# A later place for GpSimd's product of step and u and its mark, and ScalarE's normalization behind its tile's side work

## The reference, cut to what matters

```python
xf = silu(conv(x @ in_proj_w.T, conv_w))            # 512 channels
delta, B, C = split(xf @ x_proj_w.T)                # rank 16, 16 states each
dt = softplus(delta @ dt_proj_w.T + b)
y = selective_scan(u=xf, dt, A, B, C, D) * silu(res)
x = layernorm(x + (y + y_backward) @ out_proj_w.T)  # first norm
...
logits = layernorm(x)*g+b  @  slot embeddings       # 1024 slots
x = layernorm(x + combine(experts(dispatch(x))))    # second norm
```

## Time and profile before

| what | value |
|---|---|
| median of 3 runs | 5855.48 us (5845.51 to 5856.24) |
| the profiled execution's own time | 5838.37 us |
| its span, first to last instruction | 5836.5 us |
| mean granted TensorE clock | 0.929 |
| busy: TensorE, VectorE, GpSimd, ScalarE | 86%, 79%, 75%, 70% of the span |
| GpSimd, dtu (L624) | 65 times, 2179 ns |
| GpSimd, g (L643) and v (L652) | 1026 and 768 times, 2369 and 2368 ns |

### The profile page before, as it was taken

One profiled execution on the slowest core, in us unless ns is written; L12 is line 12 of the kernel. 1 busy time (PEld: TensorE's weight loads), 2 busy tenths in 40 slices (PEclk: granted clock), 3 DMA queues, 4 the chain that ended last, 5 costly groups with the idle time before them and its releaser, 6 DMA issues. The chain is left out here.

```text
span 5836.5 us, 50669 instructions
## 1 busy us (share of the span) xinstructions
PE 5031.1 (86%) x14640; PEld 2563.0 (44%) x14640; DVE 4622.5 (79%) x4109; ACT 4081.5 (70%) x6431; POOL 4362.3 (75%) x2136
## 2 busy tenths in 40 slices
PE   6888888888888888888888878787889787999999
PEld 3444443434343434344444434343434344656578
DVE  6898989898989898989898989898989992222235
ACT  4888888888888888888888888887878883111100
POOL 4898989898989999999999999999998981000000
PEclk8999989898989999999898989898989898999999
DMA  2444434444444444444444444344444442343356
GB/s 88 128 133 127 136 124 134 128 133 128 133 129 129 132 133 131 129 128 133 126 131 128 135 127 134 127 132 131 124 138 124 137 126 78 99 138 122 98 171 216
DMA packets 555604, 755.29 MB, mean 129 GB/s; under 512 B 124091, under 2 KB 272443, under 8 KB 553277
## 3 DMA queue, kind: packets, MB, share of 16 engines
q1 hardware_dynamic: 540765, 737.36, 41.1%
q10 hardware_dynamic: 14560, 14.68, 0.8%
HBM read 662.04 MB, written 89.82 MB: 129 GB/s over the span
## 5 line engine op out<-in xcount | busy, mean ns | idle before, releaser
L643 POOL TENSOR_TENSOR g_ring<-dtu,b_ring 128x1024 f32<-128x1024 f32 x1026 | 2418.9, 2369 | 271.6 <-DVE e_ps L1000 246.1
L1000 DVE TENSOR_TENSOR_SCAN e_ps<-e_ps,g_ring 128x1024 f32<-128x1024 f32 x1024 | 2343.3, 2288 | 11.8 <-POOL g_ring L643 11.8
L1156 PE MATMUL y_ps<-v_ring,ident 128*128 128x512 f32 x3088 | 1626.3, 636 | 235.1 <-DVE res_gate L983 189.9
L652 POOL TENSOR_TENSOR v_ring<-z_ring,c_ring 128x1024 f32<-128x1024 f32 x768 | 1816.7, 2368 | 0.0
L796 ACT ACTIVATE e_ps<-dt,a_neg 128x512 f32<-128x512 f32 x2050 | 1327.9, 680 | 458.1 <-DVE v_own L1022 298.3
L806 ACT ACTIVATE f_ring<-rsum,consts,a_neg_half 128x512 f32<-128x512 f32 x2052 | 1550.9, 805 | 36.7 <-DVE e_ps L1013 33.7
L1156 PEld LDWEIGHTS y_ps<-v_ring,ident 128*128 128x128 f32 x3088 | 589.3, 204 | 889.6 <-issue 807.4
L1013 DVE SCALAR_TENSOR_TENSOR z_ring<-f_ring,e_ps 128x1024 f32<-128x1024 f32 x768 | 935.6, 1218 | 50.8 <-issue 1.7
L1156 PE MATMUL y_ps<-v_own,ident 128*128 128x512 f32 x1028 | 533.8, 614 | 0.0
L1089 PE MATMUL side<-u,conv_diag 128*128 128x512 f32 x1088 | 494.6, 597 | 20.7 <-ACT disp_ring L757 11.3
L1326 ACT ACTIVATE x_act<-x_ps,x_bg 128x512 f32<-128x512 f32 x128 | 87.9, 687 | 570.2 <-PE x_ps L1385 570.2
(11 more groups left out here) (133 smaller groups left out, 5180.1 us busy)
## 6 DMA issues: line engine op xcount, KB each, us to landing
b_ring<-bc_scr SPq DMA_DIRECT2D x1027, 256.0 KB, 3.7
c_ring<-bc_scr SPq DMA_DIRECT2D x1025, 256.0 KB, 3.4
pT_scr<-rowT_ring SPq DMA_DIRECT2D x136, 256.0 KB, 4.1
m_pT<-pT_scr SPq DMA_DIRECT2D x16, 2048.0 KB, 8.5
sT_scr<-sT_ring SPq DMA_DIRECT2D x272, 64.0 KB, 2.8
x_xT<-sT_scr SPq DMA_DIRECT2D x16, 1024.0 KB, 9.3
eo_scr<-x_eo SPq DMA_DIRECT2D x32, 512.0 KB, 5.1
m_eo<-eo_scr ACTq DMA_DIRECT2D x14, 1024.0 KB, 7.1
```

The lines of the kernel that those rows point to most:

```text
L643: pool.tensor_tensor(g_ring[:, k], dtu[d][:], both(b_ring[:, k:k + 1]), ALU.mult).then_inc(g_done, 1)
L652: pool.tensor_tensor(v_slot(i), z_ring[:, k], both(c_ring[:, k:k + 1]), ALU.mult).then_inc(v_pool, 1)
L1000: dve.tensor_tensor_scan(e, e, g, 0.0, ALU.mult, ALU.add).then_inc(scan_done, 1)
L1156: pe.matmul(y_ps[:, t % 2], ident[:], v, start=(t % (TILES // PAIRS) < 2), stop=True, skip_group_check=True).then_inc(v_used, 1)
```

## The change

The product dtu is issued four tiles behind its slot and the mark six tiles behind it (three and five before). At tile 29 ScalarE goes through the side work first and normalizes behind it.

```diff
-    DTU_LAG, RSUM_LAG, CUT_LAG = 3, 3, 5
+    DTU_LAG, RSUM_LAG, CUT_LAG = 4, 3, 6
...
                     if t == ROUGH_TILE:
                         rough_rstds(b)
+                    for s in range(SLOTS):
+                        side_step(at, s, t - tile_of[s])
                     if t == APPLY_TILE:
                         normalize(b)
-                    for s in range(SLOTS):
-                        side_step(at, s, t - tile_of[s])
```

## The result

The changed kernel takes 5798.62 us (median of 4 runs, 5796.90 to 5799.63) against 5852.56 for the kernel before (5845.51 to 5856.24): a ratio of 0.9909, 95% interval 0.9892 to 0.9926. That is 54 us less where 29.7 were forecast, and 2.4 us under the low end of the range. The profiled executions stand 40.0 us apart.

What follows compares the result with a forecast made beforehand. A loop across GpSimd, ScalarE, VectorE and TensorE, 297.0 us a round, was taken as the bound; 1.5 + 0.48 = 1.98 us, times 15, is 29.7, so 5855.5 - 29.7 = 5825.8 us, range 5801 to 5849.

Steps and rivals of the forecast that it cites:

- no wait ahead of dtu: GpSimd's 4.86 us wait for the softplus ahead of dtu of dt0_1 would be nearly gone.
- 3.34 back ahead of g(53): About 3.3 of GpSimd's 4.86 us would come back as a wait for VectorE ahead of g(53).
- normalize without a wait: ScalarE's wait for GpSimd's last norm instruction ahead of normalize would be gone or below 0.2 us.
- 1.13 ahead of scan(16): VectorE's wait for the tanh would go, and one of about 1.2 us for ScalarE would appear ahead of scan(16).
- 0.55 more at the row maximum: VectorE's wait at the row maximum, which hangs on TensorE's rows, would grow by half a microsecond.
- the two other products: On GpSimd, the later dtu of dt0_3 and of dt1_1 were each taken at nothing.
- The sum of the chain: Everything behind ScalarE's normalize comes 1.5 (GpSimd's lead) + 0.48 (the tanh) = 1.98 us earlier in each of fifteen sequences.
- The second rival, a lost lead: GpSimd's lead never reaches normalize; only the tanh's slot is left, 0.48 x 15 = 7 us, 5848; chance 0.19.
- TensorE's clock: TensorE's two speed levels, looked at in in0 (5.40 or 3.70 us), were taken to give no change.
- the first rival: TensorE gets faster on top: in0 at its quick level in every sequence, 25 us more, 5801; chance 0.13.
- against the median the sum is 5855.5 - 29.7: The profiled execution lay 17.1 us below its kernel's median; the forecast against the median was 5825.8.
- sequence 0, for which I counted nothing: A dt0_1 of the loop lies ahead of normalize only in sequences 1 to 15, so sequence 0 got no gain.

Runs made afterwards that it cites:

- the order alone: Kernel before with only normalize moved behind the side work, the lags left at 3 and 5: 5827.89 us, ratio 0.9965.
- before_again: The kernel before, run unchanged for a second profile: 5846.76 us, ratio 1.0001.
- the fed kernels: Kernel before and changed kernel, each with zero-weight products ahead of six pieces of TensorE's side work: first pair 5744.19 and 5726.09 us.
- before_fed: Kernel before plus zero-weight products ahead of six pieces of TensorE's side work: 5744.19 us, ratio 0.9809.
- after_late11: Changed kernel plus one more VectorE maximum over 1024 columns in each sequence, result unused: 5823.76 us, ratio 0.9949.
- before_fed2: Kernel before plus zero-weight products, more than in before_fed ahead of xnT_0 (6 for 5) and rows_0 (7 for 4): 5742.45 us, ratio 0.9822.

## Why the prediction was wrong

**What held.** Every step about the order came out: no wait ahead of dtu, 3.34 back ahead of g(53) (3.3), normalize without a wait, 1.13 ahead of scan(16) (1.2), 0.55 more at the row maximum (0.5), the two other products worth nothing that can be measured. The sum of the chain, 1.98 us a sequence, is 2.05 by VectorE's waits. The second rival, a lost lead, is the order alone: 0.63 us by the waits where I had 0.48, and a time that is 19 us under before because the y gate shortened there too.

**The step that failed** is "TensorE's clock": "I take no change". It gave 0.95 us a sequence between before_again and after, 14 us in all. I looked for it at in0 alone, and there the first rival had the mechanism right and the place wrong: in0 came to 3.70 in only 1 of sequences 3 to 14. What shifted was the y gate behind slots_2, for which I had read no row. The trace of the kernel before held it: in those twelve sequences in0 took 5.4 in each, but the y gate waited 3.9 in three and 5.2 to 5.6 in nine, and the periods ran from 295.2 to 297.0, of which I read one, 297.0. The argument against that rival, that a gap of 2.07 was the same at both levels, was no argument: equal gaps with both levels behind them say that something else decides, and so that a shift of 2 us may change the level. What decides it these runs do not show. The rule of the Trainium skill (TensorE: Matmul & The Clock Gate, What's actually happening), that the low clock is the default and recent activity releases it, agrees with the fed kernels: rows_0 went from 3.75 in before_again to 1.96 in most sequences of before_fed, with products in the gap ahead.

**The offset.** A second step failed beside it: "against the median the sum is 5855.5 - 29.7" carried the 17.1 us between the profiled execution and the median over to the changed kernel. The changed kernel's profiled execution lies 0.3 us under its median. Of the 27.4 us by which 5826.0 was missed this is 16.8; the other 10.3 (the rest is rounding) lie between the profiled executions. Those 17.1 us were a low execution of the kernel before and a median of three on the high side: in the later sets of runs, on three chips, the medians were 5846.8, 5848.9 and 5853.4, and the second profile equals the first of these. From the span of before_again to that of after it is 48.4 us, of which 15 x 2.05 = 31 are the chain's and 14 the clock's; some 2.4 are sequence 0, for which I counted nothing (its dtu of dt0_1 comes 0.75 later, though it stands 3.1 later in its order: 1216.45 against a scan(50) at 1209.40, and 1218.76 against 1214.81 before). Of these 2.4, 1.6 are again the y gate (5.50 to 3.92) and 1.0 an earlier first scan. The last microsecond, and why the runs of before spread over 18 us and those of after over 3, are left open; that the number of sequences with the short y gate differs from run to run would explain it, but only two profiles of before stand behind that.

## What to carry to other kernels

Read a loop across the engines as a chain, and a wait taken out of it can be priced from one trace: here 1.98 us was forecast and 2.0 to 2.3 were measured. But where TensorE runs at two levels in one kernel, a shift of 2 us also moves its slow stretches. Here that was worth from half as much again to as much again, and it can also cost: 25.1 us for 19.4 us of added work in after_late11. So look at every place where VectorE or another engine waits for TensorE, and give that a term with both signs. To measure such a change by itself, make TensorE's times alike in both kernels first.

## What the runs showed that was not expected

Work that computes nothing made both kernels faster. The 22 products in each sequence of before_fed2 take 318.8 / 16 = 19.9 us of TensorE's busy time, most of it out of its gaps: between 1000 and 4600 us TensorE stands idle for 29 us a sequence in place of 44 in before_again. And the period falls from 296.50 to 289.98: rows_0 from 3.75 to 1.98, in0 from 5.40 to 3.70, the first piece of slots_2 from 3.78 to 2.05, the y gate's wait from 5.28 to 2.58. Together with the change that is 5704.5 us against 5848.9 for the kernel before on the same chip, where the change alone brings a ratio of 0.9909 and the products alone 0.9822.
